# A 32-step triangular solve on VectorE becomes two 16-step solves side by side, with the block between them made by TensorE, under a new written order

## The reference, cut to what matters

```python
A = jnp.einsum('bhncd,bhned->bhnce', kbc, kc)       # 32 x 32 per chunk
T = eye + jnp.tril(A, -1)
inv = jax.scipy.linalg.solve_triangular(T, eye, lower=True, unit_diagonal=True)
u = inv @ vc
w = inv @ kbc
def step(S, xs):                                    # over the 4 chunks of a sequence
    q_i, k_i, u_i, w_i = xs
    att = jnp.where(strict, 0.0, jnp.einsum('bhcd,bhed->bhce', q_i, k_i))
    u_adj = u_i - jnp.einsum('bhck,bhkd->bhcd', w_i, S)
    o = jnp.einsum('bhck,bhkd->bhcd', q_i, S) + att @ u_adj
    return S + jnp.einsum('bhck,bhcd->bhkd', k_i, u_adj), o
```

## Time and profile before

| | us |
|---|---|
| three runs | 1011.92, 1015.66, 1016.79 |
| median | 1015.66 |
| the profiled execution's own time | 1015.0 |
| its span, first to last instruction | 1013.2 |
| mean granted TensorE clock | 0.958 of full |
| TensorE / VectorE / ScalarE / GpSimd busy | 940.2 / 731.4 / 653.3 / 334.9 |

### The profile page before, as it was taken

How to read it: one execution, slowest core, us unless ns; L and a number is a source line. 1 busy time by engine, 2 the same in 40 slices (tenths; PEclk the granted TensorE clock), 3 DMA queues, 4 the chain that set the end, 5 groups by cost and what they waited for, 6 DMA issues and landing times.

```text
span 1013.2 us, 22026 instructions
## 1 busy us (share of the span) xinstructions
PE 940.2 (93%) x7958; PEld 601.1 (59%) x7958; DVE 731.4 (72%) x2866; ACT 653.3 (64%) x1531; POOL 334.9 (33%) x720
## 2 busy tenths in 40 slices
PE   7988999999995879999999999999977889999996
PEld 4777675645432546668776756565334555777675
DVE  2565769899998876857563688777899996764624
ACT  4498989886553235677987778566543246778743
POOL 3766323633322011537322422141240022433222
PEclk9799999999997699999999999999986999999998
DMA  9400000121353221100000000103543210000001
GB/s 314 164 1 1 1 2 11 43 53 43 95 121 65 58 54 32 43 11 22 1 13 1 1 12 22 45 9 84 115 106 74 62 36 11 11 12 1 11 1 32
DMA packets 77692, 45.44 MB, mean 45 GB/s; under 512 B 53008, under 2 KB 68880, under 8 KB 77328
## 3 DMA queue, kind: packets, MB, share of 16 engines
q1 hardware_dynamic: 77584, 44.04, 16.5%
HBM read 33.01 MB, written 11.01 MB: 43 GB/s over the span
## 4 chain that ended last, share of the span: by engine, by line
PE 69%; DVE 16%; ACT 7%; DMA 2%; POOL 2%; issue 2%; SPq 1%; ACTq 0%; POOLq 0%; DVEq 0%
PE psum L1102 7%; PE psum L995 7%; PE psum L921 6%; PE psum L559 6%; PE psum L1092 3%; PE psum L860 3%; PE psum L832 3%; PE psum L834 3%; DVE pool L1583 3%; PE psum L1086 3%; PE psum L1088 3%; DVE sol_t L1588 3%; PE psum L568 2%; ACT pool L1818 2%; ACT pool L2023 2%
## 5 line engine op out<-in xcount | busy, mean ns | idle before, releaser
L1804 ACT ACTIVATE pool<-psum 128x512 f32<-128x512 f32 x144 | 83.3, 596 | 58.1 <-PE psum L921 27.9
L1818 ACT ACTIVATE pool<-pool,small 128x128 f32<-128x128 f32 x224 | 91.6, 484 | 38.3 <-POOL small L2185 38.1
L559 PE MATMUL psum<-sb_const,pool 128*128 128x128 f32 x672 | 99.1, 282 | 9.6 <-ACT pool L1818 2.8
L921 PE MATMUL psum<-pool,firw 128*32 128x512 f32 (+7 forms) x960 | 106.4, 578 | 0.1
L2180 POOL TENSOR_SCALAR small<-small 128x4 f32<-128x4 f32 x88 | 22.2, 252 | 249.9 <-DVE small L1174 247.8
L559 PEld LDWEIGHTS psum<-sb_const,pool 128*128 128x128 f32 x672 | 78.3, 145 | 38.3 <-issue 19.0
L2183 POOL TENSOR_TENSOR small<-small,minus_half 128x4 f32<-128x4 f32 x88 | 92.3, 1049 | 7.3
L995 PE MATMUL psum<-pool,sb_l1a 128*128 128x512 f32 x192 | 92.1, 632 | 2.1 <-ACT pool L1804 2.1
L1102 PEld LDWEIGHTS psum<-sb_l1f,pool 128*128 128x128 f32 x640 | 78.3, 192 | 15.6 <-issue 13.9
L1102 PE MATMUL psum<-sb_l1f,pool 128*128 128x128 f32 x640 | 83.5, 278 | 0.0
L1405 DVE TENSOR_TENSOR pool<-pool,psum 128x512 f32<-128x512 f32 x80 | 52.7, 681 | 38.7 <-ACT pool L2090 16.6
(11 more groups left out here) (428 smaller groups left out, 2146.4 us busy)
## 6 DMA issues: line engine op xcount, KB each, us to landing
pool<-scratch_kk SPq DMA_DIRECT2D x18, 256.0 KB, 3.7
pool<-in_cF SPq DMA_DIRECT2D x16, 256.0 KB, 3.3
scratch_kk<-pool SPq DMA_DIRECT2D x10, 256.0 KB, 2.6
pool<-in_xF SPq DMA_DIRECT2D x8, 256.0 KB, 6.1
pool<-in_x SPq DMA_DIRECT2D x8, 256.0 KB, 6.2
scratch_xt<-pool SPq DMA_DIRECT2D x8, 256.0 KB, 2.0
pool<-scratch_xt SPq DMA_DIRECT2D x8, 256.0 KB, 3.2
scratch_kk<-pool SPq DMA_DIRECT2D x32, 64.0 KB, 2.0
```

The costliest lines, as they stand in the source:

```text
L559: m = e.transpose(f.ap[:, part(b)], src[:, part(b)], ident)
L921: m = e.matmul(b4(f.ap)[32 * c:32 * c + 32, :, 4 * kg:], firw[:, col, :], vsh[:, c, :, 0:P - 4 * kg], start=n == 0, stop=n == len(kgs) - 1)
L1804: e.activation(slot(g, i), f.ap, ACT.Copy).then_inc(f.emptied, 1)
L1818: m = e.activation(dst[:, part(b)], src[:, part(b)], ACT.Identity, bias=v["nm"][:, b:b + 1], scale=v["r"][:, b:b + 1])
```

## The change

The 32 x 32 lower triangle is cut into four 16 x 16 blocks. The two diagonal blocks are inverted side by side: partitions 0 to 63 hold the first one of each of the 64 triangles, partitions 64 to 127 the second. So `b_x` has 15 steps of two instructions (30 parts instead of 62), and step k works on k+1 columns of 15-k entries.

The block between, minus (second inverse) times (the 16 x 16 block of A) times (first inverse), comes from TensorE in three new steps. `b_i1` transposes the inverses (4 transposes) and ScalarE copies them to `turned`. `b_i2` multiplies keys' products by the first inverse (64 matmuls, 16 rows by 32 columns, 16 columns moving) and ScalarE copies it with a minus sign into slot 14, in 4 instructions. `b_i3` multiplies that, with unit rows beside it, by what is known of the inverse (64 matmuls, 32 x 32 by 16), and ScalarE copies the result into slot 12. `b_u` now waits for `b_i3`.

The copy of unit columns on VectorE goes; GpSimd gets a memset and a copy (in `b_sol`) and a copy of unit rows (in `b_rs`). `b_sol` reads 16 x 16 blocks, in runs of 64 bytes, half the bytes of before. `b_xo` writes runs of 128 bytes as before, and `b_xt` reads runs of 2 KB where it read runs of 128 bytes. The filters and all other arithmetic are as before. The whole text `ORDER` is a new one, in all stages.

```diff
-        tile, sol = sb(f"small{i_}", [P, 940]), sb(f"sol_t{i_}", [P, 160])
+        tile, sol = sb(f"small{i_}", [P, 940]), sb(f"sol_t{i_}", [P, 64])
+    def blocks(g):
+        both = slot(g, 12, 2)
+        return both[:, 0:3 * CB * CB].rearrange("p (m i) -> p m i", i=3 * CB), both[:, 3 * CB * CB:].rearrange("p (j i) -> p j i", i=CB)
...
         def b_sol(g, k):                                            # SyncE
-            for h in range(2):
-                e.dma_start(slot(g, 13, 2)[64 * h:64 * h + 64], dram["kk"][g]).then_inc(*chunks(g))
+            for d in range(2):
+                d_ = slice(CB * d, CB * d + CB)
+                src = dram["kk"][g].rearrange("r (j i) -> r j i", i=CH)[:, d_, d_]
+                e.dma_start(blocks(g)[1][HALF * d:HALF * d + HALF], src).then_inc(*chunks(g))
...
+        def b_i1(g, k):                                             # TensorE
+            chunked(o, g, "turned")
+            turn(begin("b_i1", g), slot(g, 12))
+        def b_i2(g, k):
+            got("b_i1", g)
+            kkt = slot(g, 8, 4).rearrange("p (q t) -> p q t", q=NP)
+            for c in range(4):
+                f, r_ = begin("b_i2", g, f"c{c}"), slice(CH * c, CH * c + CB)
+                for b in range(GB):
+                    for h in range(NH):
+                        m = e.matmul(f.ap[CH * h:CH * h + CH, CB * b:CB * b + CB], kkt[r_, h * GB + b, CH * c:CH * c + CH],
+                                     turned[r_, b * NH + h, :], start=True, stop=True)
+                m.then_inc(f.filled, 1)
+        def b_i3(g, k):
+            for c in range(4):
+                got("b_i2", g, f"c{c}")
+            o.wait_ge(sem("unit_beside"), g + 1)
+            f = begin("b_i3", g)
+            for n in range(NP):
+                for h in range(NH):
+                    h_ = slice(CH * h, CH * h + CH)
+                    m = e.matmul(f.ap[h_, CB * n:CB * n + CB], hd(slot(g, 14))[h_, n, :], by_chunk_row(g)[h_, n, CB:],
+                                 start=True, stop=True)
+            m.then_inc(f.filled, 1)
         def b_u(g, k):
-            chunked(o, g, "turned")
+            got("b_i3", g)
...
         def b_x(g, k):                                              # VectorE
-            nm, ni = k // 2 + 1, CH - 1 - k
+            nm, ni = k + 1, CB - 1 - k
             if k == 0 and not second:
                 chunked(o, g, "triangles")
-                e.tensor_copy(slot(g, 12), wt("const", "unit_rows")).then_inc(*o.link())
+                o.wait_ge(sem("units_laid"), g + 1)
...
+        def b_i1(g, k):                                             # ScalarE
+            e.activation(turned[:, :, :], hd(f.ap)[:, :, 0:CB], ACT.Copy).then_inc(f.emptied, 1)
+        def b_i2(g, k):
+            for c in range(4):
+                f = full("b_i2", g, f"c{c}")
+                e.activation(by_chunk[:, c, :, 0:CB], f.ap[:, 0:GB * CB].rearrange("p (b m) -> p b m", m=CB), ACT.Copy,
+                             scale=-1.0).then_inc(f.emptied, 1)
+        def b_i3(g, k):
+            e.activation(by_chunk_row(g)[:, :, CB:], f.ap[:, 0:NP * CB].rearrange("p (n i) -> p n i", i=CB), ACT.Copy).then_inc(f.emptied, 1)
...
+        def b_sol(g, k):                                            # GpSimd
+            e.memset(rows.rearrange("p m (z i) -> p m z i", i=CB)[:, :, 0::2, :], 0.0)
+            e.tensor_copy(rows[:, :, CB:2 * CB], unit[:, :, :]).then_inc(*mark("units_laid", g + 1))
+        def b_rs(g, k):
+            o.wait_ge(sem(f"rhs{g % NA}"), 80 * (g // NA) + 16)
+            e.tensor_copy(hd(slot(g, 14))[:, :, CB:], later[:, :].unsqueeze(1).to_broadcast([P, NP, CB])).then_inc(*mark("unit_beside", g + 1))
```

More of the change, by code:

```diff
@@ L29 @@
 CH = 32
+CB = CH // 2
 NP = NH * GB
@@ new lines @@
+f_d.2/3 b_x.18-21/0 c_nb/7 c_park/7 b_vT/2 b_ks/2 b_x.22-25/0 b_qs/2 b_k2/2 b_fir.3/1 b_q2/2 b_gg/1 b_kk/1 b_x.26-29/0
+b_xo/0 b_ag/1 b_xt/0 f_d.3-5/3 f_out/3 f_na/3 b_sol/1 b_x.0-2/1 b_fir.0-2/2 b_tr/3 b_ss/2 b_i1/0 b_v/3 b_vs/3 b_x.3/1
+b_rs/0 b_qn/2 b_x.4/1 b_gg/2 b_x.5-6/1 b_rl/0 b_x.7-8/1 b_sh/3 b_ez/3 b_x.9-14/1 b_i2/0 b_x.15/1 b_fir.3/2 b_i3/0
+b_u.0/0 b_q/3 b_x.16-17/1 b_kk/2 b_ag/2 b_fir.0/3 b_x.18-19/1 b_p.0/0 b_fir.1/3 b_k/3 b_x.20-26/1 b_u.1/0 b_qs/3
+b_q2/3 b_sol/2 b_x.0-5/2 b_x.27-28/1 b_x.6-10/2 b_vT/3 b_fir.2-3/3 b_p.1/0 b_u.2/0 b_x.11-12/2 b_x.29/1 b_ks/3 b_xo/1
@@ new lines @@
+b_xt/1 b_x.13-15/2 b_k2/3 b_ss/3 b_qn/3 b_gg/3 b_kk/3 b_p.2/0 b_u.3/0 b_x.16-19/2 b_rs/1 b_rl/1 a_load/2 b_x.20-27/2
+b_at/0 b_ag/3 b_sol/3 b_i1/1 b_x.28-29/2 b_xo/2 b_i2/1 b_us/0 b_i3/1 b_u.0/1 b_p.0/1 b_x.0-1/3 b_u.1/1 b_p.1/1
+b_x.2-6/3 b_rs/2 b_x.7/3 b_o/0 b_u.2/1 b_x.8-11/3 b_xt/2 b_i1/2 b_oT/0 b_i2/2 b_x.12-14/3 b_p.2/1 b_oF/0 b_at/1 b_i3/2
+b_x.15-16/3 b_u.3/1 b_x.17-20/3 b_rl/2 b_u.0/2 b_x.21-24/3 a_load/3 b_x.25-29/3 b_r.0-1/0 b_xo/3 b_xt/3 b_us/1 b_o/1
+b_p.0/2 b_lg/0 b_u.1/2 b_oT/1 b_lt/0 b_w/0 b_oF/1 b_p.1/2 b_i1/3 b_rs/3 b_mx.0-3/0 b_r.0/1 b_ac/0 b_u.2/2 b_ms/0
@@ new lines @@
+b_x.0-9/7 b_xo/6 b_x.10-16/7 b_xt/6 b_r.0/4 b_p.1/5 b_rs/6 b_i1/6 b_x.17-19/7 b_u.2/5 b_x.20-24/7 b_rl/6 b_i2/6
+b_x.25-26/7 b_p.2/5 b_at/5 b_x.27-29/7 b_u.3/5 b_r.1/4 b_i3/6 b_lg/4 b_xo/7 b_us/5 b_o/5 b_u.0/6 b_lt/4 b_oT/5 b_p.0/6
+b_w/4 b_xt/7 b_i1/7 b_oF/5 b_u.1/6 b_mx.0-1/4 b_rs/7 b_i2/7 b_p.1/6 b_rl/7 b_mx.2-3/4 b_u.2/6 b_ac/4 b_ms/4 b_r.0/5
+b_p.2/6 b_at/6 b_r.1/5 b_on/4 b_nF/4 b_u.3/6 b_us/6 b_i3/7 b_wo/4 b_o/6 y_k/4 b_u.0/7 b_oT/6 b_lg/5 b_p.0/7 b_oF/6
+b_u.1/7 b_lt/5 b_w/5 b_mx.0/5 b_na/4 b_r.0/6 b_p.1/7 b_mx.1/5 y_tr/4 b_mx.2-3/5 b_u.2/7 b_ac/5 b_ms/5 b_r.1/6 b_p.2/7
@@ L170 @@
     BANKS[_name, 0] = [(f"h{_k}", (_name, 0)) for _k in range(NH)]
+BANKS["b_i2", 0] = [(f"c{_k}", ("b_i2", 0)) for _k in range(4)]
 for _k in range(6):
```

224 lines of the change are left out of this document (112 added, 112 removed).

## The result

The changed kernel takes 1046.28 us (median of 4 runs, 1039.29 to 1051.25), the kernel before 1013.79 beside it: a ratio of 1.031 with an interval of 1.025 to 1.038. It is slower by 3%; the prediction said 1004, within 976 to 1030. The profiled execution spans 1044.3 us at a mean clock of 0.951 (before 1013.2 and 0.958).

The account below looks back on a forecast made before the run. TensorE was taken as the bound, with idle time and low clock in the two solve stages. Span 1013.2 + 27.8 added TensorE work - 39.0 won back = 1002.0 us, about 1004 as measured, range 976 to 1030.

Parts of the forecast that it names:

- VectorE's 79.9 us less: Solve on VectorE: busy and gaps fall from 134.7 to 54.8 us, some 54 us of it in the two solve stages.
- So of 64.4 us, 25.4 stay and 39.0 come back.: TensorE, two solve stages: of 39.1 us idle and 25.3 us lost to the lower clock, 39.0 us are won back.
- nothing moves: Rival, chance 0.17: solve-stage stalls come from the b_u and b_p chain, not a late VectorE; 28 us back, 1015.5 us.
- I count at nothing, within 5 us either way: New order of the start, the end and 400 to 700 us: no effect, as TensorE is full there with the same work.
- SyncE's transfers: Reads of triangles and transfers of inverses by SyncE: counted as 0 us in the sum.
- TensorE's 27.8 us: Inverse steps on TensorE: 3.5 us a group, 27.8 us added in all, bounds 15.7 and 48.6 us.
- 15 hand-overs at 1.3 us: TensorE's uncovered waits for copies between b_i1, b_i2, b_i3, b_u.0 and the walk: 19.5 us of idle time stay.
- The rival of 1037 us: Between b_i1 and b_u.0, 24 hand-overs hold TensorE's queue 1.35 us each, adding 32.4 us; chance 0.16.
- Small matmuls cost twice: Rival, chance 0.05: 25 ns floor for each of 256 TensorE instructions a group, 54.7 us in all, 1031 us.
- What was announced as a sign of error: Wrong if solve-stage TensorE idle stays near 40 us, its clock at 0.83 to 0.89, or full stages change over 5 us.

Follow-up runs that it names:

- e9: Changed kernel without its inverse steps (block between the two inverses left out), on the order of the kernel before: 995.5 us, ratio 0.979 to 0.986.
- e7: Changed kernel on its own new order with the three inverse steps taken out (block between left out): 1027.5 us, ratio 1.009 to 1.017.
- e4: Changed kernel on its own order, inverse steps' matmuls and copies kept but fed from constants, without link waits (block between left out): 1048.8 us.
- e3: Kernel before, its order and TensorE work kept, VectorE's solve cut to the changed kernel's 15 steps, rest of the inverse left out: 1004.3 us.
- e10: Kernel before with the chain of b_u and b_p cut (both read constants, neither waits for the other), all instructions kept: 1014.3 us.
- e11: Kernel before with the short solve (rest of the inverse left out) and the chain of b_u and b_p cut: 1001.7 us.
- e1: Whole changed kernel, links included, on the order of the kernel before, inverse steps placed ahead of each group's first b_u: 1067.7 us.
- e12: Changed kernel without inverse steps (block between left out), new order up to group 3's last b_us, then the order of before: 1013.8 us.
- e13: Short solve on before's order, inverse steps fed from constants without links, moved to stages where TensorE is full (block between left out): 1029.0 us.
- e6: Short solve on before's order, inverse steps fed from constants without links, ahead of b_u in the solve stages (block between left out): 1041.5 us.

## Why the prediction was wrong

The loss, in steps that each have a run: 1013.2 us before; 995.5 with the short solve and its frame (17.7 back, e9); 1027.5 on the new order (32.0 lost, e7); 1048.8 with the inverse steps' instructions (21.3 lost, e4); 1046.3 with the links (2.5 less, within the spread). The terms hold along this path: on the old order the same instructions cost 46 us and the links 26. In TensorE's own time, from the pages of the profiled executions:

| kernel | span | busy | idle | clock |
|---|---|---|---|---|
| before | 1013.2 | 940.2 | 73.0 | 0.958 |
| e9 | 993.7 | 931.7 | 62.0 | 0.972 |
| e7 | 1028.6 | 950.0 | 78.6 | 0.953 |
| after | 1044.3 | 972.1 | 72.2 | 0.951 |

- **VectorE's 79.9 us less.** The solve's two groups are 240 instructions of 209 ns, as announced, and their busy time fell by 72.6 us where 73.6 were forecast. The size was right; all of VectorE is busy for 67.4 us less, as other groups of it grew. The idle time before the solve's instructions, though, went from 12.1 to 25.8 us and not to 5.8, 18.8 of it in waits for the triangles.
- **"So of 64.4 us, 25.4 stay and 39.0 come back."** This is the step that failed. The short solve alone gives back 9 us (e3), the whole frame 18 (e9), and in the changed kernel 4 of the 64.4. I had read the earlier trace rows as a chain held by a late VectorE, from one row of 3.90 us. The row names who came last, and taking that one away (solve in e3, chain in e10, both in e11) let the next come last. The "nothing moves" rival was near in the little that comes back and had its cause wrong: it isn't the chain u-p-u alone either. What sets the length of the stage stays open; it is not any one of these.
- **"I count at nothing, within 5 us either way": the new order.** It costs 32 us on the kernel without inverse steps and gives 21 to the complete one (e1 against after). The wrong part was to look only at stages in which TensorE is full, and to take an order as something apart from what is in it. Both halves of the groups lose (e12), and by the marks of e7 and e9 7 us are behind before the first solve. Nor was 0 right for SyncE's transfers: with GpSimd's laying of the unit rows they seem to make the 9 us between e3 and e9, in the kernel's favour.
- **TensorE's 27.8 us.** The matmuls and transposes last 25.4 us at the full clock (e13): the working from the earlier trace rows held. Their price is 21.3 us on the new order, 33.4 in full stages and 46 in the solve stages of the old order. That the clock would be lower with them (0.953 in e6, 0.972 in e9), and the pauses without a releaser, weren't in the sum at all.
- **15 hand-overs at 1.3 us.** On the new order the links cost nothing that can be told (e4); `b_i2`'s and `b_i3`'s waits for ScalarE's copies are 0.9 and 0.7 us in all. With the waits of `b_u` and `b_p` for small copies (3.4, 3.1 and 1.0 us) that is 9.1 us in 14 waits, 0.65 each, where 19.5 were forecast. The rival of 1037 us came nearest in time, but by a mechanism that isn't there on this order; on the old one it is, with 26 us (e1 against e6).
- **Small matmuls cost twice.** 128 rows in 1.26 to 1.31 us, 10 ns each, or 20 for one float32 matmul of two rows. A floor of 25 ns, which the prediction took up, doesn't show in these rows even if it is counted for two of them; the measurement decides.
- **What was announced as a sign of error** came true in part. TensorE's clock stayed low in the first stage (0.82), but not in the second (0.92). Its idle time in the solve stages fell from 39.1 to 31.1 us, where about 20 were forecast. The full stages changed by 4.9 us ahead of the first keys' products and 3.1 between the solve stages, each under the 5 us that were named; from `b_at` of group 7 to the end, 8.7 us less go by.
- **Can the algorithm win?** e9 without the inverse steps is 18 us under before. The steps last 25.4 us on the engine that is the bound. 995.5 + 25.4 = 1021 us, an estimate for steps that cost no more than they last and links that cost nothing: still slower. No run here beat the kernel before with the whole result computed. An order fitted to the new work might do better than these two; none was made.

## What to carry to other kernels

Before you trade work of a waiting engine for work on the bound one, take the waiting engine's work away alone: here it was worth 9 us for 67, while the work added to the bound engine cost between 0.8 and 1.8 times its length. Look at the shape and number of the instructions added to the bound engine, not only at their time; a few wide matmuls were cheaper here than many small ones that last two thirds as long. A wait that a row names is the last of several: take it away and measure before you price it. Compare a new order only with the work that it was made for, and exchange both before you blame either.
